# A graph attention layer on one core: the table of summed projections and the linear logit columns are taken out, and sums move to TensorE

## What is computed

```python
h   = relu(layernorm(x))
xl  = (h @ W_n2m.T) @ Wl.T + bl            # 6250 x 128, 8 heads of 16
xr  = (h @ W_n2m.T) @ Wr.T + br
ea  = edge_attr @ W_r2m.T
loop_attr = segment_sum(ea, dst) / max(deg, 1)          # one added loop edge per node
e   = concat([ea, loop_attr]) @ We.T
u   = leaky_relu(xl[src] + xr[dst] + e, 0.2)
logits = (u * att).sum over each head
alpha  = softmax of logits over the edges of one target
out    = segment_sum(xl[src] * alpha, dst) + bias
result = x + out @ W_m2n.T
```

## Time and profile before

| | us |
|---|---|
| median of 3 runs | 2538.52 (2536.74 to 2545.29) |
| profiled execution | 2540.56 |
| its span, first to last instruction | 2538.8 |

### The profile page before, as it was taken

How to read it: one execution, slowest core, us unless ns; L and a number is a source line. 1 busy time by engine, 2 the same in 40 slices (tenths; PEclk the granted TensorE clock), 3 DMA queues, 4 the chain that set the end, 5 groups by cost and what they waited for, 6 DMA issues and landing times. The chain is left out here.

```text
span 2538.8 us, 69346 instructions
## 1 busy us (share of the span) xinstructions
PE 2292.0 (90%) x16472; PEld 1772.3 (70%) x16473; DVE 1536.3 (61%) x4344; ACT 1399.4 (55%) x4365; POOL 1708.0 (67%) x1801
## 2 busy tenths in 40 slices
PE   2468899999999999999999999999999999999665
PEld 1345677777777777777777777777777777777554
DVE  4782556565666566556656665666566566656476
ACT  1352556565666566556656655566566556665522
POOL 1137777777777777777777777777777777776013
PEclk9988999999999999999999999999999999999667
DMA  6234344443444344434444444344444434442055
GB/s 191 64 92 117 85 96 99 98 99 94 100 99 99 95 99 100 98 96 98 100 97 100 99 96 94 99 99 99 97 100 97 98 96 99 99 99 69 1 146 161
DMA packets 306919, 251.61 MB, mean 99 GB/s; under 512 B 169239, under 2 KB 278264, under 8 KB 306482
## 3 DMA queue, kind: packets, MB, share of 16 engines
q1 hardware_dynamic: 246110, 128.97, 20.9%
q0 software_dynamic: 55232, 114.70, 18.6%
q10 hardware_dynamic: 5140, 3.04, 0.4%
HBM read 231.64 MB, written 17.31 MB: 98 GB/s over the span
## 5 line engine op out<-in xcount | busy, mean ns | idle before, releaser
L788 POOL DMA_INDIRECT xl_g<-xl_table,src_tab x1708 | 1636.8, 958 | 534.9 <-issue 512.2
L865 PE MATMUL banks<-msg,onehot 128*128 128x177 f32 x3416 | 646.3, 333 | 48.4 <-DVE acc L993 47.5
L865 PEld LDWEIGHTS banks<-msg,onehot 128*128 128x128 f32 x3416 | 529.7, 194 | 216.9 <-issue 150.4
L1000 DVE SCALAR_TENSOR_TENSOR uT<-banks,relu 128x256 f32<-128x256 f32 x854 | 328.3, 420 | 488.8 <-ACT relu L920 416.4
L910 ACT ACTIVATE distance<-iota_n,minus_slot 128x128 f32<-128x128 f32 x1708 | 544.2, 390 | 26.5 <-PE banks L865 23.8
L820 PE MATMUL banks<-ident,xl_g 128*128 128x128 f32 x3416 | 503.0, 291 | 34.1 <-DMA xl_g<-xl_table,src_tab 33.7
L888 ACT ACTIVATE rbfT<-banks 128x128 f32<-128x128 f32 x427 | 118.5, 278 | 729.6 <-PE banks L801 722.3
L979 DVE TENSOR_TENSOR msg<-xl_g,banks 128x512 f32<-128x512 f32 x427 | 293.9, 688 | 330.2 <-PE banks L865 222.6
L820 PEld LDWEIGHTS banks<-ident,xl_g 128*128 128x128 f32 x3416 | 420.7, 194 | 89.8 <-DMA xl_g<-xl_table,src_tab 43.5
L810 PE MATMUL banks<-onehotT,xr_parts 128*128 128x256 bf16 x2562 | 355.4, 275 | 10.4 <-DVE uT L1000 5.7
L920 ACT ACTIVATE relu<-banks 128x256 f32<-128x256 f32 x854 | 282.7, 373 | 83.2 <-PE banks L820 73.6
(11 more groups left out here) (194 smaller groups left out, 1588.4 us busy)
## 6 DMA issues: line engine op xcount, KB each, us to landing
slot_bc<-slot_dram SPq DMA_DIRECT2D x427, 128.0 KB
rbf<-in_edge_attr SPq DMA_DIRECT2D x854, 32.0 KB
xl_g<-xl_table,src_tab POOLq DMA_INDIRECT x1708
masks<-masks_dram SPq DMA_DIRECT2D x864, 12.1 KB
x_sb<-in_x SPq DMA_DIRECT2D x6, 1024.0 KB, 17.4
x_in<-in_x SPq DMA_DIRECT2D x6, 896.0 KB, 7.5
out<-result SPq DMA_DIRECT2D x6, 896.0 KB, 5.1
both_table<-both SPq DMA_DIRECT2D x49, 68.0 KB, 1.6
```

The source lines that it names most:

```text
L788: pool.indirect_dma_start(out=xl_g[:, k % RING, t], out_offset=None, in_=xl_table, in_offset=bass.IndirectOffsetOnAxis(ap=src_tab[:, e:e + ...
L865: mm = nc.tensor.matmul(U_ps[h], onehot[:, j % 2, t], msg[:, j % 2, t], start=i == 0, stop=i == PT - 1)
L1000: nc.vector.scalar_tensor_tensor(out=uT[:, s % 2, h * PIECE:(h + 1) * PIECE], in0=z_ps[h], scalar=SLOPE, in1=relu[:, h], op0=ALU.mult, op1 ...
```

## The change

- `both_table`, `both`, POOL's addition and SP's second DMA per window are gone, and so are the logit columns: Wall has four blocks of 128, the projections 256 columns. lr_bias comes from a matmul of ones with `lr_row`, put ahead of the tables' work on PE.
- In the node loop hT is copied by ACT instead of DVE, and the high and middle parts of xr by POOL instead of ACT.
- In the last stage z is summed on PE: per window a matmul of the identity with xl_in, three with xr_parts (bf16) and the one with meanT. ACT makes 0.8 relu(z), DVE makes 0.2 z + that, times att, summed over heads.
- The two weights are first divided by the total (`shares`), then old and own are scaled with them, and PE adds the two while it transposes: two fp32 matmuls per window with the identity in the place of one transpose.
- y has four banks, so both portions follow without a wait; DVE adds x from PSUM, one turn later. POOL has no work in this stage. The stage is written out without a rolled loop.

The diff, cut to its core:

```diff
-            for w, s, r in sweep(pool, 0, WRING, WINDOWS, WINDOWS, WRING, WRING):
-                pool.wait_ge(lr_ready, w + 1)
-                if inside(w - WRING, WINDOWS):
-                    pool.wait_ge(lr_out[s], r * 32)
-                nc.gpsimd.tensor_tensor(both[:, s], lr_sb[:, s, 0:ROW], lr_sb[:, s, ROW:], ALU.add
-                                        ).then_inc(both_ready, 1)
+            for w, s, r in sweep(pool, 0, WRING, WINDOWS - 2, WINDOWS + 1, WRING, WRING):
+                if inside(w, WINDOWS):
+                    pool.wait_ge(lr_ready, w + 1)
+                    nc.gpsimd.tensor_copy(parts_of(xr_parts, w, 0), lr_sb[:, s, D_MSG:]).then_inc(hi_ready, 1)
+                if inside(w - 1, WINDOWS):
+                    pool.wait_ge(rest_ready, w)
+                    nc.gpsimd.tensor_copy(parts_of(xr_parts, w - 1, 1), rest[:, (s - 1) % WRING]).then_inc(mid_ready, 1)
...
# scalar, node loop
-                    nc.scalar.activation(parts_of(xr_parts, w - 1, 0), lr_sb[:, (s - 1) % WRING, ROW:ROW + D_MSG], ACT.Copy
-                                         ).then_inc(hi_ready, 1)
...
+                if inside(w + 1, WINDOWS):
+                    act.wait_ge(hT_done, w + 2)
+                    if inside(w - 1, WINDOWS):
+                        act.wait_ge(proj_done, w)
+                    nc.scalar.activation(hT[:, (s + 1) % 2], hT_ps[(s + 1) % 2][:, 0:2 * P], ACT.Copy
+                                         ).then_inc(hT_ready, 1)
...
# tensor
-            pe.wait_ge(w_share, 1)
+            pe.wait_ge(w_copied, 4)
...
# vector, before the node loop
+            nc.vector.tensor_copy(Wall[:].rearrange("p b d -> p (b d)"), wps[0]).then_inc(w_copied, 1)
+            nc.vector.tensor_copy(Wc[:], wps[1][:, 0:D_MSG]).then_inc(w_copied, 1)
+            nc.vector.tensor_copy(att_bc[:], wps[1][:, D_MSG:2 * D_MSG]).then_inc(w_copied, 1)
-            nc.vector.tensor_tensor(Watt[:], Wall[:, :, 0:D_MSG], att_bc[:].unsqueeze(1).broadcast_to([P, 7, D_MSG]),
-                                    ALU.mult).then_inc(w_att, 1)
...
+            nc.vector.tensor_copy(lr_bias[:], wps[1][:, 2 * D_MSG:4 * D_MSG]).then_inc(w_copied, 1)
...
# finale, tensor (T_ps, z_ps, y_ps: 2, 2 and 4 banks)
+                    pe.wait_ge(xl_loaded[n % 2], (n // 2 + 1) * 16)
+                    if n:
+                        pe.wait_ge(u_done, n)
                     for i in range(FB):
-                        mm = nc.tensor.matmul(z_ps[:, i, 0:ROW], meanT[:, i], Wc[0:D_RBF, :],
-                                              start=True, stop=True)
+                        w = n * FB + i
+                        nc.tensor.matmul(z_ps[:, i], ident[:], xl_in[:, n % 2, i], start=True, stop=False)
+                        for part in range(PARTS):
+                            nc.tensor.matmul(z_ps[:, i], ident16[:], xr_parts[:, w, part], start=False, stop=False)
+                        if i == 0:
+                            pe.wait_ge(meanT_ready, n + 1)
+                        mm = nc.tensor.matmul(z_ps[:, i], meanT[:, i], Wc[0:D_RBF, :], start=False, stop=True)
                     mm.then_inc(z_done, 1)
...
+                    pe.wait_ge(old_done, b + 1)
+                    pe.wait_ge(own_done, b + 1)
+                    pe.wait_ge(meanT_ready, min(n + 1, FBATCH))
                     for i in range(FB):
-                        mm = nc.tensor.transpose(T_ps[:, i], gat[:, i], ident[:])
+                        nc.tensor.matmul(T_ps[:, i], old[:, b % 2, i], ident[:], start=True, stop=False)
+                        mm = nc.tensor.matmul(T_ps[:, i], own[:, b % 2, i], ident[:], start=False, stop=True)
                     mm.then_inc(gatT_done, 1)
                     pe.wait_ge(gatT_ready, b + 1)
+                    if b:
+                        pe.wait_ge(result_ready, 2 * b)
+                    for lo, hi in halves:
                         for i in range(lo, hi):
-                            mm = nc.tensor.matmul(y_ps[:, i - lo], gatT[:, i], W_outT[:], start=True, stop=True)
+                            mm = nc.tensor.matmul(y_ps[:, i], gatT[:, i], W_outT[:], start=True, stop=True)
                         mm.then_inc(y_done, 1)
...
# finale, scalar
+                    act.wait_ge(z_done, n + 1)
+                    if n:
+                        act.wait_ge(u_done, n)
+                    nc.scalar.activation(relu_z[:], z_ps[:, 0:FB], ACT.Relu, scale=1.0 - SLOPE).then_inc(relu_done, 1)
...
# finale, vector: one turn is means(n); total_old, total, inv_total, shares, old, own of b; results(b - 1);
# then u, u_att, loop_logit, top, falls of n
+                    nc.vector.tensor_tensor(result[:, b % 2, lo:hi], y_ps[:, lo:hi], x_in[:, b % 2, lo:hi], ALU.add
+                                            ).then_inc(result_ready, 1)
...
+                    nc.vector.tensor_tensor(shares[:], weights[:],
+                                            inv_total[:].unsqueeze(1).broadcast_to([P, 2, FB, HEADS]), ALU.mult
+                                            ).then_inc(shares_done, 1)
...
-                    nc.vector.tensor_tensor(z[:], z_ps[:, 0:FB, 0:ROW], both_in[:, n_s], ALU.add).then_inc(z_added, 1)
+                    nc.vector.scalar_tensor_tensor(out=u[:], in0=z_ps[:, 0:FB], scalar=SLOPE, in1=relu_z[:],
+                                                   op0=ALU.mult, op1=ALU.add).then_inc(u_done, 1)
```

More of the change, by code:

```diff
@@ L179, in prologue @@
         x_sb = sb("x_sb", [P, WINDOWS, D_NODE])
[L180 to L181 removed]
+        lr_sb = sb("lr_sb", [P, WRING, 2 * D_MSG])
+        lr_bias = sb("lr_bias", [P, 2 * D_MSG])
         rest = sb("rest", [P, WRING, D_MSG])
[L183 removed]
         pads = sb("pads", [META_ROWS - PIECES, 3, PIECE], I32)
@@ L458, in _ @@
                              ).then_inc(w_prod, 1)
+            nc.tensor.matmul(wps[1][:, 2 * D_MSG:4 * D_MSG], ones[0:1, :], lr_row[:], start=True, stop=True
+                             ).then_inc(w_prod, 1)
             for c, r in enumerate(chunk_rows):
@@ L1083, in finale @@
         weights = sb("weights", [P, 2, FB, HEADS])
-        old = sb("old", [P, FB, D_MSG])
-        own = sb("own", [P, FB, D_MSG])
-        z = sb("z_loop", [P, FB, ROW])
-        two = sb("two", [P, FB, D_MSG])
-        gat = sb("gat", [P, FB, D_MSG])
         total_old = sb("total_old", [P, FB, HEADS])
@@ new lines, in results @@
+            def results(b):
+                for half, (lo, hi) in enumerate(halves):
+                    dve.wait_ge(y_done, 2 * b + half + 1)
+                    if half == 0:
+                        dve.wait_ge(x_loaded[b % 2], (b // 2 + 1) * 16)
+                        if b >= 2:
+                            dve.wait_ge(written[b % 2], (b // 2) * 16)
+                    if half and b == FBATCH - 1:
+                        dve.wait_ge(tail_loaded, 16)
+                    nc.vector.tensor_tensor(result[:, b % 2, lo:hi], y_ps[:, lo:hi], x_in[:, b % 2, lo:hi], ALU.add
+                                            ).then_inc(result_ready, 1)
@@ L1260, in _ @@
+            for b in range(-1, FBATCH):
+                n = b + 1
+                if n < FBATCH:
+                    means(n)
+                if b >= 0:
                     dve.wait_ge(weights_done, b + 1)
-                    nc.vector.tensor_tensor(total_old[:], sums[:, :, :, D_HEAD], weights[:, 0], ALU.mult
+                    nc.vector.tensor_tensor(total_old[:], sums_of(b)[:, :, :, D_HEAD], weights[:, 0], ALU.mult
                                             ).then_inc(told_done, 1)
-                    nc.vector.tensor_tensor(heads(old[:]), sums[:, :, :, 0:D_HEAD], spread(weights[:, 0]), ALU.mult
-                                            ).then_inc(old_done, 1)
@@ L1273, in _ @@
-                    dve.wait_ge(own_done, b + 1)
-                    nc.vector.tensor_tensor(two[:], old[:], own[:], ALU.add).then_inc(two_done, 1)
-                    dve.wait_ge(two_done, b + 1)
                     dve.wait_ge(itotal_done, b + 1)
-                    if inside(b - 1, FBATCH):
-                        dve.wait_ge(gatT_done, b)
-                    nc.vector.tensor_tensor(heads(gat[:]), heads(two[:]), spread(inv_total[:]), ALU.mult
-                                            ).then_inc(gat_done, 1)
```

269 lines of the change are left out of this document (98 added, 171 removed).

## The result

The changed kernel takes 2562.36 us (median of 18 runs, 2544.49 to 2572.61), the kernel before 2542.97 (18 runs, 2536.74 to 2549.34). The ratio is 1.0073, with a 95% interval of 1.0058 to 1.0087: slower by 0.7%. The prediction of 2536.7 us, with a range from 2521 to 2560, is wrong. It started from the 2538.52 us of three runs; with 18 runs the kernel before stands at 2542.97, so 4.4 of the 25.7 us that are missing come from the start value and the rest from the change.

What follows compares the result with a forecast made beforehand. DVE bounded prologue and last stage before; PE was to bound the last stage after. Prologue -14.9 us and last stage +13.1 (10.0 plus 3.1 for the clock) make -1.8, from 2538.52 to 2536.7 us; range 2521 to 2560.

Steps and rivals of the forecast that it cites:

- Prologue, set-up: Before the node loop: PE is let go earlier, lr_sb(0) starts near 97.6 instead of 102.46; gain 4.9 us.
- Prologue, loop: Node loop: a window takes 1.17 us (1.09 to 1.35) instead of 1.377, PE the largest; gain 9.9 us.
- Rival D: Node loop: POOL's copies block DVE, subtractions take 0.5 us, gain 1.8 instead of 9.9; 2544.8 us; chance 0.11.
- z, 0.71 us a window: Last stage on PE: matmuls of 0.27, three of 0.07 and 0.24 us per window; 4.5 us a batch.
- Shares, 3.8: Last stage on PE: 14 matmuls of 0.27 us a batch replace seven transposes; 3.8 us.
- rival C: Last stage: fp32 matmuls take 0.22 us, batch 13.4, no clock fall; node loop 1.09 us; 2521 us; chance 0.22.
- A batch 14.9: Last stage: PE's work and waits sum to 14.9 us per batch against 13.4 before.
- Start, 34.6 us to the third transposes: Beginning of the last stage: low clock for four windows of z(0), then full; 34.6 us to the third transposes.
- One fall of the clock, 3.1 us: Last stage: one fall in all, 6.8 us at half clock holding about 3.7 of full-clock work; 3.1 us lost.
- Tail, 16.3: End of the last stage: last shares, gatT, y, last half of results and 6.9 us to the span's end; 16.3 us.
- Rival B: Last stage: clock stays as uneven as now, mean 0.71, PE's work takes 17.2 us a batch; 2558.6 us; chance 0.21.
- The other value of the prediction, 2533.6: Last stage: if transposes don't count as busy, shares as plain matmuls hold the clock, saving 3.1 us; 2533.6 us.

Runs made afterwards that it cites:

- experiment 7: Kernel before with its mean (meanT) padded to 128 rows with zeros: ratio 1.0008, last part 118.3 us against 116.7.
- experiment 3: Changed kernel without the three bf16 matmuls of xr_parts in z: last part 152.7 us, a window 0.83 us at the full clock.
- edit 2: Changed kernel with meanT padded to 128 rows, 96 of them zero, and Wc used whole: ratio 0.9949, last part 119.0 us.
- experiment 8: Changed kernel with meanT over 128 rows, and old and own added by DVE and transposed once: ratio 0.9958, last part 123.7 us.
- 4: Changed kernel with z's windows in pairs, the 128-row matmuls of two before their 32-row ones: ratio 0.9983, last part 127.3 us.
- experiment 6: Changed kernel with z in wide matmuls and meanT padded to 128 rows: ratio 0.9907, last part 113.2 us.
- experiment 1: Changed kernel with z's xl and xr terms in matmuls over four or three windows, then the 32-row ones together: ratio 0.9946, last part 114.8 us.

## Why the prediction was wrong

Step by step:

- *Prologue, set-up*, 4.9 us: lr_sb(0) at 97.98 against 97.6 foretold, 4.5 us. Right.
- *Prologue, loop*, 1.17 us a window with a range of 1.09 to 1.35: measured 1.109. PE is the largest, as said, but I added 0.08 for the loop's overhead and a close ACT, and nothing of that showed. 12.9 us instead of 9.9. With 1.1 instead of 0.5 behind the loop the whole is 18.4 instead of 14.9. Rival D did not happen: both subtractions take 0.28 to 0.29. The exclusion that it rests on is there, but the subtraction starts first and POOL's cast is what takes longer, 0.39 instead of 0.29, on an engine with time to spare. In the last windows the cast starts first, and there the subtraction takes 0.38 (147.65 us) and the cast 0.29.
- *PE becomes the bound of the last stage*: right. DVE waits 69.0 us for relu_z there, and that for PE.
- *z, 0.71 us a window*: this step failed. I priced each matmul from a block of its own kind: 0.27 from eight records (four matmuls) of L820, 0.24 to 0.26 from a block of seven of meanT's, and added them (the terms as written make 0.72). These prices were not too low: with no change of the row count the window takes 0.67. What the sum lacks is a term for the two changes from 128 rows to 32 and back that every window has. I put it at nothing; it is 0.33 us a window (1.00 less 0.67), 2.3 us in seven. The rows that I used could hardly show it. L820's 1.09 us are 4 x 0.22 and 0.21 more, and it stands behind a block over 64 rows and ahead of matmuls with 64 columns; that these changes are the 0.21 is argued, no run takes them away. meanT's 1.85 us hold no sign of it: the same block over 128 rows takes 1.86 (experiment 7).
- *Shares, 3.8*: 3.2 (0.22 a matmul, as rival C said). gatT's wait 1.1 to 1.3 and y 3.1: right.
- *A batch 14.9*: 15.95 at the full clock. From transposes to z's end 8.33 instead of 6.5 (+1.8), shares with the wait 4.49 instead of 5.1 (-0.6), y 3.13 instead of 3.3 (-0.2).
- *Start, 34.6 us to the third transposes*: 46.06 (2404.29 to 2450.35), 11.5 more. I let the clock come up after four windows of z(0); it came up after z(1), in the shares. With 128 rows it does come up within z(0), and the third transposes are 31.5 us behind the stage's start (3463.28 to 3494.78 in the second run of that kernel).
- *One fall of the clock, 3.1 us*: three, of 4.54 us each (20.49 less 15.95), 13.6 us. I looked for the cause of falls among PE's waits, and counted PE as dense in z. The records say it is, while the granted clock falls. The runs say that the falls go with the row changes: 14 a batch, falls in three of five full batches; 8, 2 or none, no fall in a full batch that has no wait of several us; 14 changes with fewer matmuls (experiment 3), a fall in each full batch.
- *Tail, 16.3*: 46.1 + 2 x 15.95 + 3 x 20.49 = 139.5, and 16.2 are left. Right.

The sum: 34.6 + 74.5 + 16.3 + 3.1 = 128.5 us foretold for the last stage, 155.7 measured; 11.5 from the start, 5 x 1.05 = 5.3 from the batches, 10.5 from the falls make 27.3. The prologue gives 3.5 back.

Rival B named 2558.6 and a mean clock of 0.71, and the measured clock is 0.75. But it gave waits as the cause, and the mechanism is another: with edit 2 the waits stay (1.10 for gatT, as before) and the clock is full. That B's number lies 4 us from the measured one is luck. Without the row changes the case would have been near C's 2521: the ratio of 0.9949 is 18 us at 3604.98, and 18 us less than 2542.97 is 2525, an estimate. The other value of the prediction, 2533.6, for shares that hold the clock because they are plain matmuls, did not come either: the clock fell three times with such shares. Whether transposes count as idle stays open (experiment 8). One reading of the kernel before was loose: `gat` ends at 2455.75, 0.95 us after POOL's additions (2454.80) and not with them; nothing in the sum hangs on it.

What stays open: how a change of row count lowers the clock. That both go together is shown by four kernels (the changed one and experiment 3 with falls in their full batches; 2 and 4 without). With the changes PE also streams a smaller part of the time, and no run holds one of the two fixed while the other moves; that the short drains count as idleness is only argued. The Trainium skill (TensorE: Matmul & The Clock Gate, A second HAM failure mode: psum-queue depth-cycling) tells of short idle times between groups of matmuls that make the clock swing, which would fit; no record here shows them, as PE is shown busy for 9.80 of 9.80 us.

## What to carry to other kernels

Price a new chain of matmuls not kind by kind but from a row in which the same kinds follow each other, and look above all for a changing number of rows: here 0.17 to 0.19 us for each change, and the clock with it. Where a small contraction must stand among full ones, put all small ones in one block, or fill them up with zero rows, which cost nothing in this kernel (0.67 us a window against 1.00). And when a batch becomes shorter, work through its transfers once more: at 12.18 us a batch they became the next bound.

## What the runs showed of the hardware

- A change between fp32 matmuls over 128 and over 32 rows costs about 0.19 us at the full clock (0.39 for two in experiment 3, 0.39 for the last two of a batch in experiment 6). Where a change of type falls together with it, the pair is worth 0.33 us against the same matmuls over 128 rows, 0.17 each (experiments 2 and 4). Changes between fp32 and bf16 at 128 rows cost some 0.06 us for two.
- At the lower clock a window of z takes 1.76 us, and 1.44 without the bf16 matmuls; both have two changes of the row count.
- PE recorded as busy throughout does not mean a full clock: 9.80 us of 9.80 busy at 0.50, and 33.35 of 41.41 at the stage's start.
- In a block of its own a 32-row fp32 matmul of 128 columns takes hardly longer than a 128-row one: seven in 1.76 us (3524.18 to 3525.94, experiment 1), of which some 0.2 us go with the changes, against seven in 1.56 over 128 rows (2441.30 to 2442.86, experiment 6).
- A DVE subtraction of two SBUF tiles and a POOL cast that start within 0.05 us of each other delay the later one by about 0.1 us, whichever it is (0.39 against 0.29 for the cast, 0.38 against 0.29 for the subtraction).
- The changed kernel's times scatter over 28 us (2544.49 to 2572.61), those of the kernel before over 13. With falls of 4.5 us each, and up to one in each batch, that much can come from their number; it was not counted over runs.
